# Second feed-forward of a two-layer kernel: the short last chunk's gate and value in one product, and every product over all 128 rows

## The chip, the cores and the metric

The kernel runs on one core of one Trainium2 chip. The metric is the device time of the whole program in microseconds (us), lower is better. TensorE (PE) multiplies, VectorE (DVE) and ScalarE (ACT) work element by element, GpSimd (POOL) and SyncE (SP) start transfers here; the five run side by side and are ordered by semaphores.

## The reference

Two layers, each an attention and a mixture of experts side by side, all in float32. The change is in the second layer's experts:

```python
H = _ffn_size(M)                                  # M = 128, H = 688
expert_inputs = jnp.einsum('GSEC,GSM->EGCM', dispatch, x)
layer_w0 = jnp.einsum('EGCM,EMH->EGCH', expert_inputs, w0_kernel)
layer_w1 = jnp.einsum('EGCM,EMH->EGCH', expert_inputs, w1_kernel)
hidden = jax.nn.gelu(layer_w0, approximate=True) * layer_w1
expert_outputs = jnp.einsum('EGCH,EHM->EGCM', hidden, wo_kernel)
```

There are 8 experts with 1024 slots each. w0 makes the gate, w1 the value, wo the output. Their inner width, 688, is five chunks of 128 and one of 48.

## The kernel before

The program is a row of stages, each a block in which every engine has its own instruction list; at a stage's end all engines meet. `ffn1_stage` is the second feed-forward. It takes the slots in two halves, and in each half the 8 experts one after the other: 16 steps of 512 slots, q = 0 to 15. Buffers are doubled by the step's parity i. The first pair of steps is written out, the rest is in a loop of pairs, and the last pair is written out again on PE and ScalarE.

A step on PE (`step`): for each of the six chunks u one product with w0 into `ps_a[u % 2]` (L1068) and one with w1 into `ps_b[u % 2]` (L1069), each 512 columns wide. In the trace these are `f1ps_a<-f1xT,f1w` and `f1ps_b<-f1xT,f1w`. Then come four transposes of the next step's input `xe` (L1058), and then the output product: for each of 4 tiles of 128 slots the six chunks of `hid` are multiplied with `wo` and accumulated in `ps_o` (L1079). A float32 product appears in the trace as two passes, so L1079 has 48 passes a step. `hrows(u)` is 128 for the first five chunks and 48 for the last: so the last L1068 and L1069 fill 48 columns of the array (written `128*48`), and every sixth L1079 uses 48 of its rows (`48*128`).

ScalarE takes the gelu of each `ps_a` into `ge` (L1107), then copies the transposed input into `xT` (L1099) and the output into `eo` (L1112). VectorE multiplies `ge` with `ps_b` into `hid` (L1135). PE starts L1079 when all six chunks of `hid` are there:

```python
pe.wait_ge(hid_ready, (q + 1) * HC)
```

SyncE loads w0, w1, wo in two pieces, and xe for the step after (L1016 to L1020, five DMAs on one semaphore, `NL = 5`), once the output product two steps back is done. PE waits for all five before the transposes. In the first pair of steps SyncE issues the copies for the next stage's attention behind the loads of experts 0 and 1. POOL stores `eo` (L1037).

Of the kernel before, what the change touches and what calls it, by code (L numbers as in the profile page):

```python
# [8 lines left out]
ALU = mybir.AluOpType  # L9
ACT = mybir.ActivationFunctionType  # L10
AX = mybir.AxisListType

P = 128
# [50 lines left out]
def up(n):  # L64

    return max(n, 0) if isinstance(n, int) else n


def rolled(eng, n, body):

    body(0)
    with eng.Fori(1, n) as i:
        body(i)
# [338 lines left out]
HID = int(8.0 * D) * 2 // 3  # L412
HID = HID + (8 - HID) % 8
HC = -(-HID // P)
# [541 lines left out]
def hrows(c):  # L956
    return min(P, HID - c * P)
# [19 lines left out]
def ffn1_stage(nc, w0_d, w1_d, wo_d, slots_dram, eo_dram, xn_all, send_ids, sent, ident, x_all, b_out, xnT_all, front, parts, one, bias_q, bias_k):  # L977
# [3 lines left out]
    GH = NG // 2  # L981
    N = GH * CAP
    PAIRS1 = 2 * E // 2
    with Pool(nc) as m:
        w0 = [m.sb(f"f1w0{i}", [P, HID]) for i in range(2)]
        w1 = [m.sb(f"f1w1{i}", [P, HID]) for i in range(2)]
        wo = [m.sb(f"f1wo{i}", [P, HC, D]) for i in range(2)]
        xe = [m.sb(f"f1xe{i}", [P, GH, D]) for i in range(2)]
        xT = [m.sb(f"f1xT{i}", [P, N]) for i in range(2)]
        ge = m.sb("f1ge", [P, 2, N])  # L990
        hid = m.sb("f1hid", [P, HC, N])
        eo = [m.sb(f"f1eo{i}", [P, GH, D]) for i in range(2)]
        ps_t = [m.ps(f"f1ps_t{i}") for i in range(2)]
        ps_a = [m.ps(f"f1ps_a{i}") for i in range(2)]
        ps_b = [m.ps(f"f1ps_b{i}") for i in range(2)]
        ps_o = [m.ps(f"f1ps_o{i}", (P, GH, D)) for i in range(2)]
        loaded = [m.sem(f"f1loaded{i}") for i in range(2)]
        xT_done, xT_ready = m.sem("f1xT_done"), m.sem("f1xT_ready")
        a_done, a_ready = m.sem("f1a_done"), m.sem("f1a_ready")
        b_done, hid_ready = m.sem("f1b_done"), m.sem("f1hid_ready")  # L1000
        o_done, o_ready = m.sem("f1o_done"), m.sem("f1o_ready")
        stored = [m.sem(f"f1stored{i}") for i in range(2)]
        biased = m.sem("f1biased")
        NL = 5
        xs_v = slots_dram.rearrange("(e g p) d -> e p g d", e=E, p=P)
        eo_v = eo_dram.rearrange("(e g p) d -> e p g d", e=E, p=P)
        full = (HC - 1) * P
        with nc.Block() as block:
            @block.sync
            def _(sp):  # L1010
                def experts(half, r):
                    for i in range(2):
                        e = r * 2 + i
                        g = slice(half * GH, (half + 1) * GH)
                        sp.wait_ge(o_done, up(half * E + e - 1))
                        sp.dma_start(w0[i][:, :], w0_d[bass.ds(e, 1)]).then_inc(loaded[i], 16)  # L1016
                        sp.dma_start(w1[i][:, :], w1_d[bass.ds(e, 1)]).then_inc(loaded[i], 16)
                        sp.dma_start(wo[i][:, 0:HC - 1, :], wo_d[bass.ds(e, 1), 0:full].rearrange("a (c p) d -> p (a c) d", p=P)).then_inc(loaded[i], 16)
                        sp.dma_start(wo[i][0:HID - full, HC - 1, :], wo_d[bass.ds(e, 1), full:HID]).then_inc(loaded[i], 16)
                        sp.dma_start(xe[i][:, :, :], xs_v[bass.ds(e, 1), :, g, :]).then_inc(loaded[i], 16)  # L1020
                    if half == 0 and isinstance(r, int):

                        send_parts(sp, front, parts, 0)
                        stack(sp, front, parts, 0, 0)

                sp.wait_ge(sent[0], 16 * NT)
                rolled(sp, E // 2, lambda r: experts(0, r))
                sp.wait_ge(sent[1], 16 * NT)
                rolled(sp, E // 2, lambda r: experts(1, r))

            @block.gpsimd
            def _(pool):
# [16 lines left out]
                for i in range(2):  # L1049
                    pool.wait_ge(stored[i], 16 * PAIRS1)  # L1050

            @block.tensor
            def _(pe):
                def transposes(R, i):
                    pe.wait_ge(loaded[i], (R + 1) * (16 * NL))
                    pe.wait_ge(xT_ready, up(R * 2 + i - 1))
                    for g in range(GH):
                        ins = nc.tensor.transpose(ps_t[i][:, g * P:(g + 1) * P], xe[i][:, g, :], ident[:, :])  # L1058
                    ins.then_inc(xT_done, 1)

                def step(R, i, last=False):
                    q = R * 2 + i
                    pe.wait_ge(xT_ready, q + 1)
                    for u in range(HC):
                        n = hrows(u)
                        pe.wait_ge(a_ready, up(q * HC + u - 1))
                        pe.wait_ge(hid_ready, up(q * HC + u - 1))
                        nc.tensor.matmul(ps_a[u % 2][0:n, :], w0[i][:, u * P:u * P + n], xT[i][:, :], start=True, stop=True).then_inc(a_done, 1)  # L1068
                        nc.tensor.matmul(ps_b[u % 2][0:n, :], w1[i][:, u * P:u * P + n], xT[i][:, :], start=True, stop=True).then_inc(b_done, 1)  # L1069
                    if not last:  # L1070
                        transposes(R + i, 1 - i)
                    pe.wait_ge(hid_ready, (q + 1) * HC)
                    pe.wait_ge(o_ready, up(q - 1))
                    if isinstance(R, int) and q == 1:
                        pe.wait_ge(front.sm["qk_ready"], 2)
                    for s in range(GH):
                        for c in range(HC):
                            n = hrows(c)
                            ins = nc.tensor.matmul(ps_o[i][:, s, :], hid[0:n, c, s * P:(s + 1) * P], wo[i][0:n, c, :],  # L1079
                                                   start=(c == 0), stop=(c == HC - 1))  # L1080
                    ins.then_inc(o_done, 1)

                def pair(R):
                    for i in range(2):
                        step(R, i)

                pe.wait_ge(front.sm["loaded"], 16 * 3)
                for n in range(2):
                    multiply_qk(nc, front, ps_o[n][:, :, :].rearrange("p (w j) d -> p w (j d)", w=2), xnT_all, n)
                transposes(0, 0)  # L1090
                rolled(pe, PAIRS1 - 1, pair)
                step(PAIRS1 - 1, 0)
                step(PAIRS1 - 1, 1, last=True)

            @block.scalar
            def _(a):
                def keep_T(R, i):
                    a.wait_ge(xT_done, R * 2 + i + 1)
                    nc.scalar.activation(xT[i][:, :], ps_t[i][:, :], ACT.Copy).then_inc(xT_ready, 1)  # L1099

                def step(R, i, last=False):
                    q = R * 2 + i
                    for u in range(HC):
                        n = hrows(u)
                        a.wait_ge(a_done, q * HC + u + 1)
                        a.wait_ge(hid_ready, up(q * HC + u - 1))
                        nc.scalar.activation(ge[0:n, u % 2, :], ps_a[u % 2][0:n, :], ACT.Gelu_apprx_tanh).then_inc(a_ready, 1)  # L1107
                    if not last:
                        keep_T(R + i, 1 - i)
                    a.wait_ge(o_done, q + 1)  # L1110
                    a.wait_ge(stored[i], R * 16)
                    nc.scalar.activation(eo[i][:, :, :], ps_o[i][:, :, :], ACT.Copy).then_inc(o_ready, 1)  # L1112

                def pair(R):
                    for i in range(2):
                        step(R, i)
                        if isinstance(R, int) and i == 0:
                            keep_qk(nc, a, front, ps_o[1][:, :, :].rearrange("p (w j) d -> p w (j d)", w=2), bias_q, bias_k, 1)

                keep_qk(nc, a, front, ps_o[0][:, :, :].rearrange("p (w j) d -> p w (j d)", w=2), bias_q, bias_k, 0)  # L1120
                keep_T(0, 0)
                rolled(a, PAIRS1 - 1, pair)
                step(PAIRS1 - 1, 0)
                step(PAIRS1 - 1, 1, last=True)

            @block.vector
            def _(v):
                def pair(R):
                    for i in range(2):
                        q = R * 2 + i  # L1130
                        for u in range(HC):
                            n = hrows(u)
                            v.wait_ge(a_ready, q * HC + u + 1)
                            v.wait_ge(b_done, q * HC + u + 1)
                            nc.vector.tensor_tensor(hid[0:n, u, :], ge[0:n, u % 2, :], ps_b[u % 2][0:n, :], ALU.mult).then_inc(hid_ready, 1)  # L1135

                rolled(v, PAIRS1, pair)


# [697 lines left out]
```

## Time and profile before

| what | value |
|---|---|
| median of 3 runs | 1888.92 us (1887.74 to 1889.97) |
| profiled execution, its own time | 1885.4 us |
| its span, first to last instruction | 1883.7 us |
| PE busy in the span | 1722.3 us (91%) |
| VectorE, ScalarE, POOL busy | 918.6, 764.0, 296.5 us |
| mean granted PE clock | 0.970 of full |
| second feed-forward in the span | from 928.6 to about 1242 us |

Times in the rows below are microseconds from the start of the span. Row by row, a group of instructions has its start, its duration from first start to last end, its engine, source line, output and inputs, and in brackets the idle time before it with what ended it. The granted clock is a share of 2.4 GHz: 1.00 or 0.50.

### The profile page before, as it was taken

Reading aid. Unit: us, or ns where it says so; the run is one execution under the profiler, and the core shown is the slowest. Engines: PE = TensorE matmul, PEld = TensorE weight load, DVE = VectorE, ACT = ScalarE, POOL = GpSimd, SP = SyncE. Lnnn points to the kernel's source line nnn. Section 1 sums busy time; section 2 is a strip of 40 time slices with the busy share of each in tenths; the row PEclk is TensorE's granted clock in tenths of the full one; section 3 lists DMA queues with packets and bytes.
Section 4 is the critical chain, followed back from the end, with each engine's and each line's share of the span. In section 5 each row is a group of like instructions: output and inputs, shape, how many; then the busy total and the mean of one; then the engine's idle time right before and its main releaser. Section 6 shows DMA issues by size and latency. Waiting matters only on the chain. (4 is left out here: it accounts for less than half of the span.)

```text
span 1883.7 us, 38993 instructions
## 1 busy us (share of the span) xinstructions
PE 1722.3 (91%) x13304; PEld 1307.1 (69%) x13304; DVE 918.6 (49%) x3193; ACT 764.0 (41%) x2111; POOL 296.5 (16%) x375
## 2 busy tenths in 40 slices
PE   3698999999999999999699999959999999999896
PEld 3466778888888888888455555537777777777775
DVE  4323554545454555555321222236767666676664
ACT  1333222222222222222222222247767677776773
POOL 1001020101010101010240000003222322232222
PEclk9899999999999999999799999979999999999998
DMA  1201920000000000000232232248777777777775
GB/s 45 60 0 13 104 60 7 12 1 12 0 11 0 11 0 11 0 11 1 74 105 83 86 94 74 73 143 230 223 220 223 200 219 214 222 220 194 225 223 159
DMA packets 228518, 181.82 MB, mean 97 GB/s; under 512 B 80287, under 2 KB 217337, under 8 KB 228336
## 3 DMA queue, kind: packets, MB, share of 16 engines
q1 hardware_dynamic: 222962, 167.14, 33.6%
q0 software_dynamic: 5376, 12.44, 2.2%
q8 instruction: 94, 1.54, 0.4%
q14 instruction: 86, 0.70, 0.1%
HBM read 103.60 MB, written 75.78 MB: 95 GB/s over the span
## 5 line engine op out<-in xcount | busy, mean ns | idle before, releaser
L757 DVE TENSOR_TENSOR a0MT<-a0ps_M,mask 128x384 f32<-128x384 f32 x256 | 142.5, 557 | 259.4 <-PE a0ps_M L606 259.3
L1561 DVE CUSTOM_DVE_ANT_0 a1Pm<-a1ps_S,a1Sb 128x256 f32<-128x256 f32 x512 | 195.9, 420 | 147.7 <-issue 143.8
L1499 ACT ACTIVATE a1Pm<-a1Pm,a1nmx 128x256 f32<-128x256 f32 x512 | 254.6, 503 | 1.3 <-DVE a1nmx L1561 1.3
L701 ACT ACTIVATE a0qk<-a0ps_qk 128x512 f32<-128x512 f32 x128 | 76.5, 597 | 423.5 <-PE a0ps_qk L582 423.5
L1494 ACT ACTIVATE a1Rt<-a1ps_R 128x384 f32<-128x384 f32 x264 | 128.9, 488 | 170.0 <-PE a1ps_R L1369 164.7
L1135 DVE TENSOR_TENSOR f1hid<-f1ge,f1ps_b 128x512 f32<-128x512 f32 x96 | 65.9, 687 | 234.4 <-PE f1ps_b L1069 234.4
L1388 PE MATMUL a1ps_T<-ident,a1Pm 128*128 128x128 f32 x1024 | 163.0, 283 | 0.0
L604 PE MATMUL a0ps_M<-a0AT 128*128 128x256 f32 x512 | 153.9, 382 | 0.0
L752 DVE TENSOR_TENSOR a0AT<-a0ps_A,mask 128x384 f32<-128x384 f32 x256 | 130.8, 552 | 37.7 <-PE a0ps_A L591 37.7
L582 PE MATMUL a0ps_qk<-xnT_all,a0w_in 128*128 (+1 forms) x512 | 144.7, 405 | 1.4 <-PEq L310 1.4
L1378 PE MATMUL a1ps_S<-a1stk 72*128 72x256 bf16 x512 | 104.0, 286 | 22.0 <-issue 22.0
L1388 PEld LDWEIGHTS a1ps_T<-ident,a1Pm 128*128 128x128 f32 x1024 | 119.1, 146 | 2.2 <-ACT a1Pm L1499 0.2
L1369 PE MATMUL a1ps_R<-rel_st,a1stk 72*128 72x192 bf16 x528 | 91.9, 258 | 28.7 <-ACT a1Rt L1494 18.1
L1079 PE MATMUL f1ps_o<-f1wo,f1hid 128*128 128x128 f32 (+1 forms) x768 | 111.6, 291 | 5.1 <-DVE f1hid L1135 5.1
L1079 PEld LDWEIGHTS f1ps_o<-f1wo,f1hid 128*128 128x128 f32 (+1 forms) x768 | 95.1, 190 | 23.1 <-DVE f1hid L1135 6.2
L605 PEld LDWEIGHTS a0ps_M<-a0AT 128*128 128x128 f32 x512 | 97.9, 191 | 13.4
L582 PEld LDWEIGHTS a0ps_qk<-xnT_all,a0w_in 128*128 128x128 f32 x512 | 86.7, 189 | 23.4 <-issue 1.5
L1068 PE MATMUL f1ps_a<-f1xT,f1w 128*128 128x512 f32 x192 | 101.7, 611 | 0.7 <-ACT f1xT L1099 0.7
L1499 ACT ACTIVATION_READ_ACCUMULATOR a1Pm<-a1Pm,a1nmx 128x1 f32 x512 | 99.4, 194 | 0.0
L606 PE MATMUL a0ps_M<-a0AT 128*128 128x128 f32 x512 | 99.1, 275 | 0.0
L1069 PE MATMUL f1ps_b<-f1xT,f1w 128*128 128x512 f32 x192 | 98.9, 597 | 0.0
L605 PE MATMUL a0ps_M<-a0AT 128*128 128x128 f32 x512 | 98.8, 275 | 0.0
(236 smaller groups left out, 3061.0 us busy)
## 6 DMA issues: line engine op xcount, KB each, us to landing
skew<-a1Rt SPq DMA_DIRECT2D x132, 384.0 KB, 3.6
a1Sb<-skew SPq DMA_DIRECT2D x131, 384.0 KB, 4.9
f1w<-in_L_ffn_w_kernel SPq DMA_DIRECT2D x32, 344.0 KB, 3.4
a1stk<-parts SPq DMA_DIRECT2D x51, 192.0 KB
a1stk<-parts SPq DMA_DIRECT2D x153, 64.0 KB
parts<-a1prt SPq DMA_DIRECT2D x18, 384.0 KB, 4.7
f1wo<-in_L_ffn_wo_kernel SPq DMA_DIRECT2D x16, 320.0 KB, 4.2
slots<-zeros SPq DMA_DIRECT2D x8, 512.0 KB, 14.9
```

The costliest lines, as they stand in the source:

```text
L582: ins = nc.tensor.matmul(ps_qk[:, i, :], w_in[:, i, p * P:(p + 1) * P], xnT_all[:, bass.ds(b * T, T)], start=True, stop=True)
L604: nc.tensor.matmul(ps_M[h][:, 0:T], AT[h][:, 0:P], AT[h][:, 0:T], start=True, stop=True)
L605: nc.tensor.matmul(ps_M[h][:, T:HB], AT[h][:, P:T], AT[h][:, P:T], start=True, stop=False)
L752: nc.vector.tensor_tensor(AT[h][:, :], ps_A[h][:, 0:HB], mask[:, :], ALU.mult).then_inc(A_ready, 1)
L757: nc.vector.tensor_tensor(MT[h][:, :], ps_M[h][:, 0:HB], mask[:, :], ALU.mult).then_inc(M_ready, 1)
L1068: nc.tensor.matmul(ps_a[u % 2][0:n, :], w0[i][:, u * P:u * P + n], xT[i][:, :], start=True, stop=True).then_inc(a_done, 1)
L1079: ins = nc.tensor.matmul(ps_o[i][:, s, :], hid[0:n, c, s * P:(s + 1) * P], wo[i][0:n, c, :], start=(c == 0), stop=(c == HC - 1))
L1378: ins = nc.tensor.matmul(ps_S[hp % 2][:, n, :], stk[par][:, 0, h, it * P:(it + 1) * P], stk[par][:, 1, h, :], start=True, stop=True)
L1388: ins = nc.tensor.transpose(ps_T[k % 2][:, n, jt, :], Pm[:, place(2 * k + n), jt * P:(jt + 1) * P], ident[:, :])
L1494: nc.scalar.activation(Rt[:, hp, :, :], ps_R[:, :, :].rearrange("p n c -> p c n"), ACT.Copy).then_inc(sm["R_ready"], 1)
L1499: nc.scalar.activation(Pm[:, place(h), :], Pm[:, place(h), :], ACT.Exp, bias=nmx[it][:, h:h + 1], scale=-1.0, accum_out=den[it][:, h:h + 1 ...
L1561: nc.vector.tensor_tensor_reduce(out=Pm[:, place(h), :], in0=ps_S[hp % 2][:, n, :], in1=bias_of(it, hp, n), scale=-1.0, scalar=3.0e38, op0 ...
```

## The change

The two weights w0 and w1 stand in one buffer `w[i]`: 688 gate columns, 16 zero columns, the last 48 value columns, then the first 640 value columns. So the 128 columns from 640 on are the last 48 of the gate, 16 zeros, the last 48 of the value, and 16 columns of the value's first chunk. The last chunk needs one product, into `ps_a`, which has gate results on partitions 0 to 47 and value results on 64 to 111. ScalarE reads its gelu from partitions 0 to 47 and writes `ge` on 64 to 111, and VectorE multiplies there and writes `hid` there. The last chunk of `wo` is loaded to the same partitions; the other rows of `wo` and `hid` in that chunk are cleared once by VectorE at the start of the stage, and L1079 multiplies 128 rows in every chunk. SyncE waits for the clearing, and has six DMAs a step instead of five.

```diff
-        w0 = [m.sb(f"f1w0{i}", [P, HID]) for i in range(2)]
-        w1 = [m.sb(f"f1w1{i}", [P, HID]) for i in range(2)]
+        w = [m.sb(f"f1w{i}", [P, 2 * HID + PAD]) for i in range(2)]
...
-        NL = 5
+        cleared = m.sem("f1cleared")
+        NL = 6
...
-                        sp.dma_start(w0[i][:, :], w0_d[bass.ds(e, 1)]).then_inc(loaded[i], 16)
-                        sp.dma_start(w1[i][:, :], w1_d[bass.ds(e, 1)]).then_inc(loaded[i], 16)
+                        sp.dma_start(w[i][:, 0:HID], w0_d[bass.ds(e, 1)]).then_inc(loaded[i], 16)
+                        sp.dma_start(w[i][:, VALUE:VALUE + full], w1_d[bass.ds(e, 1), :, 0:full]).then_inc(loaded[i], 16)
+                        sp.dma_start(w[i][:, HID + PAD:VALUE], w1_d[bass.ds(e, 1), :, full:HID]).then_inc(loaded[i], 16)
-                        sp.dma_start(wo[i][0:HID - full, HC - 1, :], wo_d[bass.ds(e, 1), full:HID]).then_inc(loaded[i], 16)
+                        sp.dma_start(wo[i][UP, HC - 1, :], wo_d[bass.ds(e, 1), full:HID]).then_inc(loaded[i], 16)
...
+                sp.wait_ge(cleared, 1)
                 sp.wait_ge(sent[0], 16 * NT)
...
-                        nc.tensor.matmul(ps_a[u % 2][0:n, :], w0[i][:, u * P:u * P + n], xT[i][:, :], start=True, stop=True).then_inc(a_done, 1)
-                        nc.tensor.matmul(ps_b[u % 2][0:n, :], w1[i][:, u * P:u * P + n], xT[i][:, :], start=True, stop=True).then_inc(b_done, 1)
+                        nc.tensor.matmul(ps_a[u % 2][:, :], w[i][:, u * P:(u + 1) * P], xT[i][:, :], start=True, stop=True).then_inc(a_done, 1)
+                        if u < HC - 1:
+                            nc.tensor.matmul(ps_b[u % 2][:, :], w[i][:, VALUE + u * P:VALUE + (u + 1) * P], xT[i][:, :],
+                                             start=True, stop=True).then_inc(b_done, 1)
...
-                            n = hrows(c)
-                            ins = nc.tensor.matmul(ps_o[i][:, s, :], hid[0:n, c, s * P:(s + 1) * P], wo[i][0:n, c, :],
+                            ins = nc.tensor.matmul(ps_o[i][:, s, :], hid[:, c, s * P:(s + 1) * P], wo[i][:, c, :],
...
-                        nc.scalar.activation(ge[0:n, u % 2, :], ps_a[u % 2][0:n, :], ACT.Gelu_apprx_tanh).then_inc(a_ready, 1)
+                        nc.scalar.activation(ge[to, u % 2, :], ps_a[u % 2][of, :], ACT.Gelu_apprx_tanh).then_inc(a_ready, 1)
...
-                            nc.vector.tensor_tensor(hid[0:n, u, :], ge[0:n, u % 2, :], ps_b[u % 2][0:n, :], ALU.mult).then_inc(hid_ready, 1)
-
+                            nc.vector.tensor_tensor(hid[rows, u, :], ge[rows, u % 2, :], values[rows, :], ALU.mult).then_inc(hid_ready, 1)
+
+                for i in range(2):
+                    nc.vector.memset(w[i][:, HID:HID + PAD], 0.0)
+                    nc.vector.memset(wo[i][:, HC - 1, :], 0.0)
+                nc.vector.memset(hid[:, HC - 1, :], 0.0).then_inc(cleared, 1)
+                v.wait_ge(cleared, 1)
```

On PE, at the end of a step in the written-out first pair, there stood before:

```order
L1068 MATMUL f1ps_a<-f1xT,f1w 128x512
L1069 MATMUL f1ps_b<-f1xT,f1w 128x512
L1068 MATMUL f1ps_a<-f1xT,f1w 48x512
L1069 MATMUL f1ps_b<-f1xT,f1w 48x512
L1058 MATMUL f1ps_t<-ident,f1xe 128x128 x4
L1079 MATMUL f1ps_o<-f1wo,f1hid 128x128 x24
```

and now the same place reads, with the changed kernel's line numbers:

```order
L1074 MATMUL f1ps_a<-f1xT,f1w 128x512
L1076 MATMUL f1ps_b<-f1xT,f1w 128x512
L1074 MATMUL f1ps_a<-f1xT,f1w 128x512
L1065 MATMUL f1ps_t<-ident,f1xe 128x128 x4
L1086 MATMUL f1ps_o<-f1wo,f1hid 128x128 x24
```

One product of the two of the last chunk is gone, and the other has 128 columns of weights. The 24 products of L1079 are as many as before (their rows of the array don't show in this listing).

On VectorE, at the start of the stage and through its first step, there stands now:

```order
L1133 UNCONDITIONAL_BRANCH
L1146 MEMSET f1w 128x16
L1147 MEMSET f1wo 128x128
L1146 MEMSET f1w 128x16
L1147 MEMSET f1wo 128x128
L1148 MEMSET f1hid 128x512
L1143 TENSOR_TENSOR f1hid<-f1ge,f1ps_b 128x512 x5
L1143 TENSOR_TENSOR f1hid<-f1ge,f1ps_a 48x512
```

The five memsets are new, and the sixth product of the step reads `ps_a` where it read `ps_b`.

On SyncE, at the start of the stage, the loads of one expert were these five:

```order
L1016 DMA f1w<-in_L_ffn_w_kernel 128x688
L1017 DMA f1w<-in_L_ffn_w_kernel 128x688
L1018 DMA f1wo<-in_L_ffn_wo_kernel 128x5x128
L1019 DMA f1wo<-in_L_ffn_wo_kernel 48x128
L1020 DMA f1xe<-slots 128x4x128
```

and are now these six:

```order
L1021 DMA f1w<-in_L_ffn_w_kernel 128x688
L1022 DMA f1w<-in_L_ffn_w_kernel 128x640
L1023 DMA f1w<-in_L_ffn_w_kernel 128x48
L1024 DMA f1wo<-in_L_ffn_wo_kernel 128x5x128
L1025 DMA f1wo<-in_L_ffn_wo_kernel 48x128
L1026 DMA f1xe<-slots 128x4x128
```

The load of w1 is in two pieces, and the input `xe` is sixth in the row instead of fifth.

## Rows read from the trace of the kernel before

**Rows 1.** The page: PE's busy time, and its granted clock in 40 slices

```profile
PE 1722.3 (91%) x13304; PEld 1307.1 (69%) x13304; DVE 918.6 (49%) x3193; ACT 764.0 (41%) x2111; POOL 296.5 (16%) x375
...
PEclk9899999999999999999799999979999999999998
```

**Rows 2.** Busy time by stretch: stretch, length, each engine's busy us, clock, DMA

```profile
932.00:935.40 3.40, 0.27 (x1) 0.00 (x0) 0.00 (x0) 0.00 (x0) 2.79 (x3) 1.00 1.05 348
935.40:942.20 6.80, 5.45 (x9) 2.56 (x10) 0.45 (x1) 2.48 (x3) 4.97 (x7) 0.50 0.59 197
...
958.40:1237.00 278.60, 272.41 (x1138) 156.91 (x1136) 61.81 (x90) 72.19 (x122) 17.42 (x22) 1.00 0.27 82
```

**Rows 3.** Waits from 925 to 1240 us: total, times, longest

```profile
PE f1ps_o L1079 <- DVE f1hid L1135: 5.1, 16, 0.8
```

**Rows 4.** Timeline of PE around a step's short chunk and L1079

```profile
1013.90 1.13 PE L1068 MATMUL f1ps_a<-f1xT,f1w 128*128 128x512 f32 x2
...
1021.72 1.02 PE L1069 MATMUL f1ps_b<-f1xT,f1w 128*128 128x512 f32 x2
1022.68 1.06 PE L1068 MATMUL f1ps_a<-f1xT,f1w 128*48 128x512 f32 x2
1023.57 1.02 PE L1069 MATMUL f1ps_b<-f1xT,f1w 128*48 128x512 f32 x2
1024.53 0.66 PE L1058 MATMUL f1ps_t<-ident,f1xe 128*128 128x128 f32 x4
1025.52 6.97 PE L1079 MATMUL f1ps_o<-f1wo,f1hid 128*128 128x128 f32 x48 [0.33 <-DVE f1hid L1135]
1032.42 1.12 PE L1068 MATMUL f1ps_a<-f1xT,f1w 128*128 128x512 f32 x2
1033.38 1.02 PE L1069 MATMUL f1ps_b<-f1xT,f1w 128*128 128x512 f32 x2
1034.24 1.02 PE L1068 MATMUL f1ps_a<-f1xT,f1w 128*128 128x512 f32 x2
```

**Rows 5.** Timeline of ScalarE and VectorE for the same short chunk

```profile
1023.77 0.59 ACT L1107 ACTIVATE f1ge<-f1ps_a 48x512 f32<-48x512 f32 x1 [1.25 <-PE f1ps_a L1068]
...
1024.70 0.68 DVE L1135 TENSOR_TENSOR f1hid<-f1ge,f1ps_b 48x512 f32<-48x512 f32 x1 [1.16 <-PE f1ps_b L1069]
```

**Rows 6.** PE elsewhere: full passes alone, full and short; then L1079's mean pass

```profile
555.06 3.73 PE L628 MATMUL a0ps_g<-a0w_out,a0oT 128*128 128x128 f32 x32
...
137.20 1.16 PE L401 MATMUL f0ps_y<-f0w,f0hw 128*128 128x128 f32 x8
138.29 0.48 PE L403 MATMUL f0ps_y<-f0b,f0wT 8*128 8x128 f32 x2
138.70 1.16 PE L401 MATMUL f0ps_y<-f0w,f0hw 128*128 128x128 f32 x8
...
L1079 PE MATMUL f1ps_o<-f1wo,f1hid 128*128 128x128 f32 x40 | 5.5, 285 | 0.3 <-DVE f1hid L1135 0.3
```

**Rows 7.** Timeline at the start of this stage and of the next

```profile
928.67 0.34 SPq L1016 DMA_DIRECT2D f1w<-in_L_ffn_w_kernel  x1
...
930.58 0.42 SPq L1020 DMA_DIRECT2D f1xe<-slots  x1
...
936.06 1.12 PE L1058 MATMUL f1ps_t<-ident,f1xe 128*128 128x128 f32 x4 [3.79 <-DMA f1xe<-slots]
...
1242.63 0.34 SPq L1224 DMA_DIRECT2D parts<-a1prt  x1
...
1243.07 1.76 DVE L1632 MEMSET a1vx<- 128x2048 f32 x1 [14.41 <-PEq L1008]
1245.00 0.91 DVE L1633 MEMSET a1Sb<- 128x1024 f32 x1 [0.16 <-issue]
```

**Rows 8.** A load of f1xe in mid-stage, and all 16 from issue to landing

```profile
1016.19 0.38 SPq L1020 DMA_DIRECT2D f1xe<-slots  x1
...
DMA to landing us min/median/max: 4.0/5.0/6.7
```

More of the change, by code:

```diff
@@ L983, in ffn1_stage @@
     PAIRS1 = 2 * E // 2
+    full = (HC - 1) * P
+    SHORT = HID - full
+    PAD = P // 2 - SHORT
+    UP = slice(P // 2, P // 2 + SHORT)
+    VALUE = HID + PAD + SHORT
     with Pool(nc) as m:
-        w0 = [m.sb(f"f1w0{i}", [P, HID]) for i in range(2)]
-        w1 = [m.sb(f"f1w1{i}", [P, HID]) for i in range(2)]
+        w = [m.sb(f"f1w{i}", [P, 2 * HID + PAD]) for i in range(2)]
         wo = [m.sb(f"f1wo{i}", [P, HC, D]) for i in range(2)]
@@ L1003, in ffn1_stage @@
         biased = m.sem("f1biased")
-        NL = 5
+        cleared = m.sem("f1cleared")
+        NL = 6
         xs_v = slots_dram.rearrange("(e g p) d -> e p g d", e=E, p=P)
         eo_v = eo_dram.rearrange("(e g p) d -> e p g d", e=E, p=P)
-        full = (HC - 1) * P
         with nc.Block() as block:
@@ L1064, in step @@
                     for u in range(HC):
-                        n = hrows(u)
                         pe.wait_ge(a_ready, up(q * HC + u - 1))
                         pe.wait_ge(hid_ready, up(q * HC + u - 1))
-                        nc.tensor.matmul(ps_a[u % 2][0:n, :], w0[i][:, u * P:u * P + n], xT[i][:, :], start=True, stop=True).then_inc(a_done, 1)
-                        nc.tensor.matmul(ps_b[u % 2][0:n, :], w1[i][:, u * P:u * P + n], xT[i][:, :], start=True, stop=True).then_inc(b_done, 1)
+                        nc.tensor.matmul(ps_a[u % 2][:, :], w[i][:, u * P:(u + 1) * P], xT[i][:, :], start=True, stop=True).then_inc(a_done, 1)
+                        if u < HC - 1:
+                            nc.tensor.matmul(ps_b[u % 2][:, :], w[i][:, VALUE + u * P:VALUE + (u + 1) * P], xT[i][:, :],
+                                             start=True, stop=True).then_inc(b_done, 1)
                     if not last:
@@ L1103, in step @@
                     for u in range(HC):
-                        n = hrows(u)
+                        to, of = (slice(0, P), slice(0, P)) if u < HC - 1 else (UP, slice(0, SHORT))
                         a.wait_ge(a_done, q * HC + u + 1)
                         a.wait_ge(hid_ready, up(q * HC + u - 1))
-                        nc.scalar.activation(ge[0:n, u % 2, :], ps_a[u % 2][0:n, :], ACT.Gelu_apprx_tanh).then_inc(a_ready, 1)
+                        nc.scalar.activation(ge[to, u % 2, :], ps_a[u % 2][of, :], ACT.Gelu_apprx_tanh).then_inc(a_ready, 1)
                     if not last:
@@ L1131, in pair @@
                         for u in range(HC):
-                            n = hrows(u)
+                            rows, values = (slice(0, P), ps_b[u % 2]) if u < HC - 1 else (UP, ps_a[u % 2])
                             v.wait_ge(a_ready, q * HC + u + 1)
-                            v.wait_ge(b_done, q * HC + u + 1)
-                            nc.vector.tensor_tensor(hid[0:n, u, :], ge[0:n, u % 2, :], ps_b[u % 2][0:n, :], ALU.mult).then_inc(hid_ready, 1)
+                            if u < HC - 1:
+                                v.wait_ge(b_done, q * (HC - 1) + u + 1)
+                            nc.vector.tensor_tensor(hid[rows, u, :], ge[rows, u % 2, :], values[rows, :], ALU.mult).then_inc(hid_ready, 1)
[4 more added lines that the diff above has]
+                v.wait_ge(cleared, 1)
                 rolled(v, PAIRS1, pair)
```

## The prediction

> **What bounds the kernel now.** I read the page first: TensorE (PE) is busy for 91% of the span and its granted clock is near full everywhere [rows 1]. The change touches only the second feed-forward. I cut the trace at its edges and at the edges of the granted clock [rows 2]: from 958.4 to 1237.0 us PE is busy 272.4 of 278.6 us, always at clock 1.00 (2.4 GHz), while VectorE is busy 61.8 and ScalarE 72.2 us. So PE sets the pace there. In the list of waits for the stage [rows 3] PE waits for f1hid only 5.1 us in all, 16 times (once a step). What PE issues, and how densely, is the time of the stage.
>
> The PE timeline of one step [rows 4] shows how it is spent. Each 128x512 product is two passes (f32), and one product starts 0.86 us after the other (1033.38 to 1034.24). The step is 12 such products, 4 transposes, 48 passes of L1079, and takes 18.52 us (1013.90 to 1032.42). Look at the starts around the short chunk: 1021.72 to 1022.68 is 0.96, to 1023.57 is 0.89, to 1024.53 is 0.96: each change of shape adds 0.03 to 0.10. Then 48 passes of L1079 run from 1025.52 to the next L1068 at 1032.42, 6.90 us, or 144 ns a pass. Dense passes of the same size are quicker: the 32 passes of L628, all 128 rows, two accumulation groups of 16, take 3.73 us from first start to last end [rows 6]; less one pass of 0.285 us (mean of L1079) that is 31 gaps in 3.45 us, 111 ns.
>
> **The change, part by part.**
>
> 1. *The short chunk's product into f1ps_o gets 128 rows.* The nearest case of a short product among full ones is L403 (8 rows) among L401 [rows 6]: 8 full and 2 short passes recur every 1.50 us (137.20 to 138.70), where ten passes at 111 ns would be 1.115. The short product costs 0.385 us more than a full one. It is the passage that costs, not the rows' number: the two short passes begin at 138.29, the next full one at 138.70, 0.41 us for two. For our step: 48 gaps, of which the first after an idle engine stays 0.21, is 47 x 0.1115 + 0.21 = 5.45 us against 6.90: 1.45 saved. The next L1068 also ends its wait behind a short shape: its two passes take 0.96 to the next product (1032.42 to 1033.38) against 0.86, 0.10 more saved. Together 1.55; the other way, 4 x 0.385 = 1.54. I take 1.55 a step.
>
> The Trainium skill has two rules here. "TensorEngine Tiling (Array Packing)", section Tiling Modes, says that a change of tiling mode drains the engine; "TensorE: Matmul & The Clock Gate", section on LDWEIGHTS, says that the number of rows does not matter to a weight load, which taken alone speaks against any gain from zero rows. By the second alone this term would be 0, by the first it is what the rows show; the trace agrees with the first, at about 0.1 us for each passage.
>
> 2. *One product instead of two for the short chunk.* On PE this removes one L1069 (0.89 us) and the 0.10 and 0.10 of the passages, 1.09 in all. Little of it can be kept: the L1079 group waits for the last f1hid. That chain is now f1ps_a, gelu, product on VectorE. From the rows of both engines [rows 5]: the gelu of the short chunk starts 1.09 after its f1ps_a product (1022.68 to 1023.77) and takes 0.59; the VectorE product takes 0.68 and PE goes on 0.14 after its end (1025.38 to 1025.52). With the product at 1022.58: gelu 1023.67 to 1024.26, VectorE (hand-over not shown here; between 0 and 0.14, I take 0.05) 1024.31 to 1024.99, L1079 at 1025.13 instead of 1025.52. Saved: 0.39; with the bounds of the hand-over 0.30 to 0.44. PE then stands idle about 1 us between the transposes and L1079, where it was 0.33. No row shows a gelu that reads partitions 0 to 47 and writes 64 to 111; nothing in the rows prices it but the 0.59 of the unshifted one. If it or the VectorE operation took its time twice, 0.6 a step would go; I take no extra cost.
>
> Per step 1.55 + 0.39 = 1.94, and 16 steps: 31.0 us.
>
> 3. *Clearing and the sixth load, at the stage's start.* SyncE now waits for five memsets before its first DMA, and PE's first transposes wait for that load [rows 7]: issued 928.67 to 930.58, used at 936.06, after 3.79 us of idle PE. At the start of the next stage VectorE begins 0.44 us after SyncE (1242.63, 1243.07). A memset of 2048 elements a partition takes 1.76 and one of 1024 0.91, so 0.83 ns an element and 0.06 for each: 16, 128, 16, 128 and 512 elements make 0.07 + 0.17 + 0.07 + 0.17 + 0.48 = 0.96; gaps of 0 to 0.16 between them (1244.83 to 1245.00) make it 0.96 to 1.6. With the 0.44 and 0.1 for the signal the loads start 1.5 to 2.1 later. The sixth DMA pushes f1xe back by one issue, (930.58 - 928.67)/4 = 0.48. So PE starts 2.0 to 2.6 later. But it starts at clock 0.50 [rows 2], until 942.2. If the clock still rises then, a delay of 2.3 loses only 1.15, since half speed is what is lost. If it rises one 3.4 us stretch later, the loss is 2.9. I take 2.0, bounds 1.1 to 2.9.
>
> 4. *Later loads.* SyncE issues six DMAs a step. f1xe was issued at 1016.19 and lands 5.0 us later in the median, 6.7 at most [rows 8]: 1021.2, at most 1022.9, for transposes at 1024.53. Now it lands 0.48 later for transposes 1.19 earlier, so 1021.7 (at most 1023.4) against 1023.34, and PE's idle microsecond hides another 0.9. This costs nothing. POOL's queue is not touched.
>
> Sum: 31.0 - 2.0 = 29.0 us. The profiled execution is 1885.4 us (span 1883.7 and 1.7 around it) and would become 1856.4; it lies 3.5 below the median of the runs, 1888.9. I put the saving against the median: 1859.9, and forecast **1860 us**.
>
> **The rivals.**
>
> - *Zero rows bring nothing*: the excess in L1079 belongs to the boundary of accumulation groups. Then only term 2 is left: 16 x 0.39 - 2.0 = 4.2, so 1884.7. For it: in L1079 the short product always stands at such a boundary, as in L403. Against: L628 has one in its 32 passes and still runs at 111 ns. 4%.
> - *The loads come late*: 128 pieces of 192 bytes more, six issues. If f1xe landed 8.5 us after its issue (1025.2), it would be 0.95 past the 1024.24 from which PE feels it: 15 us lost, 1875. Nothing in the landing times of before (6.7 at most) reaches there. 5%.
> - *The clock falls, and it gets slower*: each step now has an idle microsecond next to the transposes. In the rows the clock was at 0.50 after PE had been nearly idle from 932.0 to 935.4 (0.27 us busy). Each microsecond at half clock costs 0.5, so the saving of a step is gone when 3.9 us of it run so. One stretch of 6.8 us in each step, as in 935.4 to 942.2, would cost 3.4 - 1.94 = 1.5 a step: 1860 + 16 x 3.4 = 1914. Against: an idle of 1 us is far below 3.4, and the rest of the step is dense. 3%.
> - *The shifted gelu or the 48-row product from f1ps_a is slow*: 0.6 a step, 1870. 6%.
>
> **How the numbers follow.** The forecast has 82%. Its own range: term 1 is known to 0.05 a step, term 2 to 0.1, together 2.4 us; the start 1; the granted clock in the attention stage that follows changes places when all moves 29 us, and a stretch of 3.4 us at half clock costs up to 1.7, a few of them more or less 3 to 4 us. That is 1854 to 1866. To take in half of the slow chain and of the late loads I give 1854 to 1870. Differences over 0.2% (3.8 us) can be told from no change. The first two and the fourth rival are all still faster (1884.7 is 0.22% below), the first of them just: faster 0.94, same 0.03, slower 0.03.
>
> **What would show it.** In the profile after: the passes of L1079 (now one form) start to next product in 5.4 to 5.5 us; a step of 16.5 us; one idle of PE near 1.0 us a step, ended by f1hid, about 16 us in all where 5.1 were; f1ps_b in 160 instead of 192 passes; first transposes near 938.4; VectorE waiting on ScalarE's f1ge 16 times; clock 1.00 throughout the steps. I would be wrong if L1079 stayed near 6.9 us, if transposes waited for f1xe in each step, or if clock 0.50 appeared between 960 and the stage's end.

## The result and the profile after

The changed kernel takes 1856.15 us (median of 4 runs, 1853.29 to 1862.72) against 1889.45 for the kernel before (4 runs). The ratio is 0.9828, 95% interval 0.9813 to 0.9844: 33.3 us faster where 29 were forecast, and inside the range of 1854 to 1870. Measured once more it was 0.985 (0.983 to 0.987), 1859.18 against 1887.12: 27.9 us faster.

The profiled execution took 1857.91 us, its span 1856.3. The page after, beside [rows 1]:

```profile
span 1856.3 us, 38958 instructions
...
PE 1681.9 (91%) x13272; PEld 1301.4 (70%) x13272; DVE 921.0 (50%) x3198; ACT 763.5 (41%) x2111; POOL 296.7 (16%) x375
...
PEclk9899999999999999999889999979999999999998
```

PE is busy 40 us less and keeps its share. The timeline of PE over one step after, beside [rows 4]:

```profile
990.23 1.02 PE L1074 MATMUL f1ps_a<-f1xT,f1w 128*128 128x512 f32 x2
991.09 1.02 PE L1076 MATMUL f1ps_b<-f1xT,f1w 128*128 128x512 f32 x2
...
997.95 1.02 PE L1076 MATMUL f1ps_b<-f1xT,f1w 128*128 128x512 f32 x2
998.81 1.02 PE L1074 MATMUL f1ps_a<-f1xT,f1w 128*128 128x512 f32 x2
999.67 0.60 PE L1065 MATMUL f1ps_t<-ident,f1xe 128*128 128x128 f32 x4
1001.24 5.62 PE L1086 MATMUL f1ps_o<-f1wo,f1hid 128*128 128x128 f32 x48 [0.97 <-DVE f1hid L1143]
1006.70 1.02 PE L1074 MATMUL f1ps_a<-f1xT,f1w 128*128 128x512 f32 x2
```

The 48 passes of the output product now take 5.46 us to the next product (1001.24 to 1006.70) where they took 6.90; the next product's passes begin 0.86 apart, not 0.96; the passages around the last chunk are gone (997.95, 998.81, 999.67: 0.86 each). This step takes 16.47 us (990.23 to 1006.70). Steps take two lengths in turn, 16.47 and 16.55, and before it was 18.45 and 18.52; the means are 16.504 and 18.477. PE now idles 0.97 before the output product. ScalarE and VectorE in the same place, beside [rows 5]:

```profile
999.87 0.59 ACT L1114 ACTIVATE f1ge<-f1ps_a 48x512 f32<-48x512 f32 x1 [1.12 <-PE f1ps_a L1074]
...
1000.49 0.69 DVE L1143 TENSOR_TENSOR f1hid<-f1ge,f1ps_a 48x512 f32<-48x512 f32 x1 [0.79 <-ACT f1ge L1114]
```

The gelu that moves partitions 0 to 47 to 64 to 111 takes 0.59 like the one that did not, and hands over to VectorE within 0.03 us. The waits of the stage after, beside [rows 3]:

```profile
PE f1ps_o L1086 <- DVE f1hid L1143: 15.4, 15, 1.4
...
PE f1ps_t L1065 <- DMA f1xe<-slots: 5.6, 2, 4.6
```

The start of the stage, beside [rows 7]:

```profile
928.75 0.07 DVE L1146 MEMSET f1w<- 128x16 f32 x1 [0.34 <-PEq L513]
928.81 0.17 DVE L1147 MEMSET f1wo<- 128x128 f32 x1
928.92 0.07 DVE L1146 MEMSET f1w<- 128x16 f32 x1
928.97 0.17 DVE L1147 MEMSET f1wo<- 128x128 f32 x1
929.19 0.48 DVE L1148 MEMSET f1hid<- 128x512 f32 x1
...
929.71 0.34 SPq L1021 DMA_DIRECT2D f1w<-in_L_ffn_w_kernel  x1
...
932.09 0.42 SPq L1026 DMA_DIRECT2D f1xe<-slots  x1
...
936.99 1.12 PE L1065 MATMUL f1ps_t<-ident,f1xe 128*128 128x128 f32 x4 [4.57 <-DMA f1xe<-slots]
```

The clearing takes 0.92 us from first start to last end, the first load is issued 1.04 later than before, f1xe 1.51 later (932.09 to 930.58), but the transposes start only 0.93 later: they come 4.9 us after the load's issue instead of 5.5. That 0.93 holds for this pair of profiles. In a second pair the transposes came 8.15 us after the stage's first product, against 6.45 before, which is 1.70 later.

### The profile page after: what moved, and what is told of

It is laid out like the page before. It is cut to its first block and busy times, and to the rows that moved or that the text cites. A ratio compares the mean times of both kernels' runs of the same rounds, so it can differ in the third digit from the quotient of the medians.

```text
span 1856.3 us, 38958 instructions
## 1 busy us (share of the span) xinstructions
PE 1681.9 (91%) x13272; PEld 1301.4 (70%) x13272; DVE 921.0 (50%) x3198; ACT 763.5 (41%) x2111; POOL 296.7 (16%) x375
## 5 line engine op out<-in xcount | busy, mean ns | idle before, releaser
L1143 DVE TENSOR_TENSOR f1hid<-f1ge,f1ps_b 128x512 f32<-128x512 f32 x80 | 55.0, 688 | 191.0 <-PE f1ps_b L1076 182.4
L1086 PE MATMUL f1ps_o<-f1wo,f1hid 128*128 128x128 f32 x768 | 89.9, 277 | 15.4 <-DVE f1hid L1143 15.4
L1086 PEld LDWEIGHTS f1ps_o<-f1wo,f1hid 128*128 128x128 f32 x768 | 87.0, 192 | 19.6 <-DVE f1hid L1143 11.9
L1418 PE MATMUL a1ps_X<-a1PT,tabs 128*128 128x256 f32 x384 | 96.1, 387 | 0.0
```

Of the source, the lines that this page charges most:

```text
L1086: ins = nc.tensor.matmul(ps_o[i][:, s, :], hid[:, c, s * P:(s + 1) * P], wo[i][:, c, :], start=(c == 0), stop=(c == HC - 1))
L1418: ins = nc.tensor.matmul(ps_X[k % 2][:, n, :, :], tabs[:, t, :], PT[it][:, jt, :, ig * GI:(ig + 1) * GI], start=(q == 0), stop=(q == len(u ...
```

## Experiments

Times are medians of 4 runs (10 for one product alone, 12 for the repeat of the kernel before). Ratios are to the kernel before, measured beside each. "Step" is the mean distance between the first products of steps 3 to 15 in the trace.

**Zero rows alone.** In the kernel before only the output product is changed, with the clearing that it needs:

```diff
-                            n = hrows(c)
-                            ins = nc.tensor.matmul(ps_o[i][:, s, :], hid[0:n, c, s * P:(s + 1) * P], wo[i][0:n, c, :],
+                            ins = nc.tensor.matmul(ps_o[i][:, s, :], hid[:, c, s * P:(s + 1) * P], wo[i][:, c, :],
```

> The kernel before, with the zero rows alone: wo and hid cleared, L1079 over 128 rows in every chunk; gate and value of the short chunk stay two products. Theory (the passages between a short and a full product are what L1079 pays): its 48 passes take about 5.45 us from first start to the next product where they took 6.90, and a step takes 18.48 - 1.55 = 16.93 us. With 0.5 us lost at the start, about 24 us faster than the kernel before. Rival (the excess sits at the boundary of accumulation groups): a step stays at 18.5 us and the time at that of before.

Its PE timeline:

```profile
1000.67 0.66 PE L1060 MATMUL f1ps_t<-ident,f1xe 128*128 128x128 f32 x4
1001.58 5.62 PE L1080 MATMUL f1ps_o<-f1wo,f1hid 128*128 128x128 f32 x48 [0.26 <-DVE f1hid L1136]
1007.04 1.02 PE L1070 MATMUL f1ps_a<-f1xT,f1w 128*128 128x512 f32 x2
1007.90 1.02 PE L1071 MATMUL f1ps_b<-f1xT,f1w 128*128 128x512 f32 x2
...
1014.77 1.02 PE L1071 MATMUL f1ps_b<-f1xT,f1w 128*128 128x512 f32 x2
1015.72 1.06 PE L1070 MATMUL f1ps_a<-f1xT,f1w 128*48 128x512 f32 x2
1016.62 1.02 PE L1071 MATMUL f1ps_b<-f1xT,f1w 128*48 128x512 f32 x2
1017.57 0.66 PE L1060 MATMUL f1ps_t<-ident,f1xe 128*128 128x128 f32 x4
1018.56 5.62 PE L1080 MATMUL f1ps_o<-f1wo,f1hid 128*128 128x128 f32 x48 [0.34 <-DVE f1hid L1136]
```

Step 16.931 us against 18.477: 1.546 less, to the hundredth the 1.55 forecast. The four group boundaries (where one accumulation ends and the next begins) are all still there and cost nothing; the rival falls. The passages of the 48-column products remain (0.95, 0.90, 0.95). Time: 1867.36 us, ratio 0.9893 (0.9867 to 0.9918), 19.2 us under the 1886.59 beside it, where 24 were expected; the stage itself is 24.2 shorter than in the first profile of before and 22.0 than in the second.

**One product alone.** The changed kernel with the short rows put back into the output product:

```diff
-                            ins = nc.tensor.matmul(ps_o[i][:, s, :], hid[:, c, s * P:(s + 1) * P], wo[i][:, c, :],
+                            k = slice(0, P) if c < HC - 1 else UP
+                            ins = nc.tensor.matmul(ps_o[i][:, s, :], hid[k, c, s * P:(s + 1) * P], wo[i][k, c, :],
```

> The changed kernel, but the output product's last chunk uses only the 48 rows 64 to 111 (same results). Theory: only the chain's gain stays, 0.42 us a step as in the trace after (its output product starts 2.43 us after the last f1ps_a product; before, 2.84 us after a product that itself stood 0.1 later): steps of about 18.0 us, in all 6 us faster than before. Rival (removing one product of 0.86 us and two passages frees PE by 1.1 us a step): 17.4 us a step, 17 us faster.

```profile
1002.59 0.60 PE L1065 MATMUL f1ps_t<-ident,f1xe 128*128 128x128 f32 x4
1004.16 6.98 PE L1087 MATMUL f1ps_o<-f1wo,f1hid 128*128 128x128 f32 x48 [0.97 <-DVE f1hid L1144]
1011.07 1.13 PE L1074 MATMUL f1ps_a<-f1xT,f1w 128*128 128x512 f32 x2
```

Step 18.052 us, 0.425 less than before: the chain's gain and no more. Of the 1.1 us that PE no longer works, 0.97 stands as idle ahead of the output product, where 0.33 were. The output product is back at 6.91. Time: 1883.29, ratio 0.9977 (0.9961 to 0.9994), 3.3 us faster where 6 were expected; the stage is 6.7 shorter than in the first profile of before, 4.5 than in the second. The two parts add up: 1.546 + 0.425 = 1.971, and the full change gives 18.477 - 16.504 = 1.973.

**112 rows instead of 128.** As the last, with `slice(0, UP.stop)` for the short chunk.

> The changed kernel, but the output product's last chunk uses rows 0 to 111 (of 128) instead of all. If what costs is the change between a product of at most 64 rows and one of more, 112 rows cost nothing: steps of 16.51 us as in the changed kernel. If every change in the number of rows costs, steps of about 18.0 us, 25 us slower than the changed kernel.

A step's output product and the next product, then the groups of the stage by shape:

```profile
1005.27 5.62 PE L1087 MATMUL f1ps_o<-f1wo,f1hid 128*128 128x128 f32 x48 [0.97 <-DVE f1hid L1144]
1010.73 1.02 PE L1074 MATMUL f1ps_a<-f1xT,f1w 128*128 128x512 f32 x2
...
L1087 PE MATMUL f1ps_o<-f1wo,f1hid 128*128 128x128 f32 x640 | 83.5, 277 | 15.4 <-DVE f1hid L1144 15.4
...
L1087 PE MATMUL f1ps_o<-f1wo,f1hid 112*128 112x128 f32 x128 | 24.7, 274 | 0.0
```

Step 16.504 us, the changed kernel's to the nanosecond; 1859.38 us, ratio 0.9849 (0.9822 to 0.9875). A product of 112 rows among products of 128 is free, one of 48 or 8 is not. Where between 48 and 112 rows the cost begins, no run here shows.

**The wait for the sixth chunk, later.** The changed kernel, where PE waits for five chunks of hid before the output product and for the sixth ahead of its first use:

```diff
-                    pe.wait_ge(hid_ready, (q + 1) * HC)
+                    pe.wait_ge(hid_ready, q * HC + HC - 1)
...
+                            if s == 0 and c == HC - 1:
+                                pe.wait_ge(hid_ready, q * HC + HC)
```

> The changed kernel, but PE starts the output product when five chunks of hid are there and waits for the sixth only ahead of the first product that reads it. Theory (after the change the chain gelu, product on VectorE is the only thing PE waits for in a step, 1.0 us): it starts right behind the transposes, about 1.1 us a step is saved, steps of 15.4 us, 17 us faster than the changed kernel. Rival (the chain sets the pace and the wait only moves on to the sixth product): half of the gain, 8 us.

```profile
1009.37 1.02 PE L1074 MATMUL f1ps_a<-f1xT,f1w 128*128 128x512 f32 x2
...
1010.23 0.60 PE L1065 MATMUL f1ps_t<-ident,f1xe 128*128 128x128 f32 x4
...
1010.66 2.51 PE L1088 MATMUL f1ps_o<-f1wo,f1hid 128*128 128x128 f32 x20
...
1011.05 0.69 DVE L1145 TENSOR_TENSOR f1hid<-f1ge,f1ps_a 48x512 f32<-48x512 f32 x1 [0.79 <-ACT f1ge L1116]
```

The output product starts 0.43 us after the transposes do, with no idle, while VectorE is still to make the sixth chunk. VectorE ends it at 1011.74, and the eleventh pass, the first that reads it, would start about 1011.8 (1010.66 and ten passes of 0.11): it comes just in time. Step 15.357 us, 1.147 less. 1840.39 us, ratio 0.9751 (0.9725 to 0.9777), and 0.9768 (0.9725 to 0.9811) when measured again. One thing shows that the cover is gone: in the second step the transposes wait for their load,

```profile
964.22 0.66 PE L1065 MATMUL f1ps_t<-ident,f1xe 128*128 128x128 f32 x4 [1.98 <-DMA f1xe<-slots]
```

and that step takes 17.44 us instead of 15.36. In the second profile of this kernel the wait was 2.35 us, the granted clock then stood at 0.50 for 3.4 us (from 967.95), and the step took 19.44. So the fall of the clock that the prediction had as a rival for every step did come, once, in another kernel; behind the wait of 1.98 us in the first profile it did not, and not behind one of 2.92 us in the kernel with all three. The changed kernel waits in the same step,

```profile
967.83 0.66 PE L1065 MATMUL f1ps_t<-ident,f1xe 128*128 128x128 f32 x4 [1.03 <-DMA f1xe<-slots]
```

and its step of 16.49 us is no longer than the others (16.47 and 16.55 in turn), since PE would have idled there. In its second profile the wait was 1.35 and the step 16.82, so there 0.35 us stuck out.

**The clearing off the load's path.** The changed kernel, but in the first step SyncE waits for the clearing only ahead of the short piece of wo.

> The changed kernel, but SyncE waits for the clearing only ahead of the one load that touches cleared rows (the short piece of wo). Theory (the clearing costs what it delays the first load): first load at 928.7 instead of 929.7, first transposes 0.5 to 1 us earlier, which at half clock is worth 0.3 to 0.9 us of the total; not to be told from the changed kernel in the timing, only in the trace. Rival (the first load of xe is bound by the transfers already queued): first transposes unchanged near 937.0.

The first transposes came 6.58 us after the stage's first product, against 8.27 in the changed kernel; but the first step took 18.94 instead of 18.39, and the whole stage 283.2 against 283.3. The timing, 1857.02 us with ratio 0.9839 (0.9803 to 0.9875), can't be told from the changed kernel's. Since the first transposes of the kernel before stand at 7.42 in one profile and 6.45 in another, these profiles do not settle how much of the 1.69 us is the clearing. They do show where the lead went: the second step took 17.54 us instead of 16.49, because its transposes waited 2.07 us for their load. SyncE issues that load behind the copies for the attention, and these begin 21.6 to 21.7 us after the stage's first product in every profile, whether PE is early or late. The awaited transposes come 39.01 us after the stage's first product here and 39.11 in the changed kernel. So time won at the stage's start is mostly waited away in its second step.

**Zero rows in the first feed-forward.** The changed kernel, where the bias product of 8 rows becomes one of 128, both operands cleared once:

```diff
-        b2s = m.sb("f0b2", [E, D])
+        b2s = m.sb("f0b2", [P, D])
...
-        wT = m.sb("f0wT", [E, GT])
+        wT = m.sb("f0wT", [P, GT])
...
+                nc.vector.memset(wT[:, :], 0.0)
+                nc.vector.memset(b2s[:, :], 0.0).then_inc(f0cleared, 1)
```

> The changed kernel, with the same zero rows for another stage: in the first feed-forward the bias product of 8 rows (L403) becomes one of 128 rows, with its two operands cleared once. Theory (0.385 us for each such product among full ones, 32 of them): 8 full and 2 former short passes recur every 1.115 us instead of 1.50, 12 us in all if PE bounds that stage; 10 to 12 us faster than the changed kernel. Rival (the stage waits for VectorE and ScalarE, the gain turns into idle of PE): the passes are quicker but the stage as long as before.

Its PE timeline, beside [rows 6]:

```profile
128.49 1.06 PE L405 MATMUL f0ps_y<-f0w,f0hw 128*128 128x128 f32 x8
129.38 0.39 PE L407 MATMUL f0ps_y<-f0b,f0wT 128*128 128x128 f32 x2
129.60 1.06 PE L405 MATMUL f0ps_y<-f0w,f0hw 128*128 128x128 f32 x8
```

Ten passes recur every 1.11 us (128.49 to 129.60) instead of 1.50. 1845.71 us, ratio 0.9786 (0.9753 to 0.9819): 10.4 less than the changed kernel's 1856.15, 13.5 less than its 1859.18, and 11.3 less than the 1857.02 of the last experiment, which was measured beside it. The traces are cleaner than the medians: from the first f0ps_y pass to the last pass of that stage it is 95.2 us in the first profiles of before and after, and 83.7 in the kernel with all three, 11.5 less, with the clock at 1.00 in each. The 10 to 12 expected hold; PE bounds that stage.

**All three together.**

> The changed kernel with the late wait for the sixth chunk, the clearing off the load's path, and the zero rows in the first feed-forward together. If the three are independent: 17 + 0.5 + 11 = 28 us faster than the changed kernel, 1828 us. If the first feed-forward gives nothing: 1839 us.

1827.56 us (1825.82 to 1828.50), ratio 0.9685 (0.9652 to 0.9718): 62.1 us under the kernel before (1889.65), and 28.6 under the changed kernel's 1856.15 (31.6 under its 1859.18), where the sum was 28. It is the fastest version found.

**What is chance.** The kernels before and after were profiled and timed again:

> The kernel before, unchanged, profiled once more. Theory (the part of a difference that lies in the attention stage at the end is chance, since the granted clock falls at other places from one execution to the next): the second feed-forward again takes 314.1 us within 0.3, the attention stage differs from the 640.9 of the first profile by some us. Rival (the attention stage is as repeatable as the rest, so its 3.4 us more in the changed kernel belong to the change): 640.9 within 0.5.

> The changed kernel, unchanged, profiled once more, against the kernel before in five rounds. Theory: the second feed-forward again takes 283.3 us within 0.5, the attention stage differs from 644.3 by some us; the ratio lies at 1 - 30.9/1887 = 0.9836 within its interval. Rival (the change costs or gives something in the attention stage): a stage of 644.3 again and a ratio off 0.9836 by more than its interval.

and two of the others:

> The kernel with the zero rows alone, unchanged, profiled and timed once more. Its first profile had 648.8 us in the attention stage, where the kernel before has 640.9 and 641.0, and its median was 19 us below the kernel before where its second feed-forward was 24 us shorter. If the attention stage is chance, it lies elsewhere this time; if it belongs to the kernel (the same code begins at another moment of the transfers), it is 648.8 within 1 again.

> The kernel with the late wait, unchanged, profiled and timed once more. Its first profile had 646.4 us in the attention stage. Chance: elsewhere between 640 and 650 this time. The kernel's own: 646.4 within 1. The second feed-forward is 266.7 us within 0.5 either way.

From all traces: the second feed-forward (first product of the stage to the first of the next), the attention stage behind it to the end, whose code is the same in all, and how long the clock was at 0.50 in that attention stage, in us:

```
kernel                  2nd feed-forward   attention   at half clock
before                       314.1           640.9         67.5
before, again                311.9           641.0         67.6
after                        283.3           644.3         70.9
after, again                 283.8           641.8         71.7
zero rows alone              289.9           648.8         82.2
zero rows alone, again       290.0           644.6         74.6
one product alone            307.4           642.7         69.3
112 rows                     283.5           647.3         77.3
late wait                    266.7           646.4         76.3
late wait, again             268.8           642.4         69.0
clearing aside               283.2           645.1         71.7
first feed-forward too       284.4           640.8         70.8
all three                    267.7           641.1         64.3
```

The attention stage moves by up to 8 us between kernels, and by 0.1 to 4.2 between two profiles of one. It is longest where the clock was longest at half: the zero rows alone had 14.7 us more of half clock than before, which by an estimate (half speed loses half the time where PE is busy) is worth up to 7.3 of their 7.9 us. The code ahead of the second feed-forward is no steadier: the eleven profiles that share it reach the stage 925.6 to 932.7 us after their start. The first feed-forward took 125.6 us in the repeats of before and after and 122.4 in their first profiles: in the repeats the clock was at 0.50 for its last 10 us.

So there is room for the few us between the gain in the stage and the gain in the median: 24.2 and 19.2 for the zero rows (20.1 when repeated), 30.9 and 33.3 for the change (28.1 and 27.9 when repeated). That they lie in these other stages is likely and not shown, since of each kernel's runs only one or two were profiled. The repeat of the kernel before came out at 1.0003 (0.9989 to 1.0018), so over a dozen runs its median repeats. For the zero rows alone both profiles lie above the 641 of before; whether that kernel draws longer stretches or had bad luck twice is open.

The expectations for the repeats were missed in three places. The second feed-forward of the kernel before took 311.9 where 314.1 within 0.3 was expected, and that of the late wait 268.8 where 266.7 within 0.5 was; the first has its cause at the stage's start, the second mainly in the clock's fall told above. And the attention stage of before, which was to differ by some us, repeated within 0.1: for this kernel the rival came true, for the other three that were profiled twice it fell.

## Why the prediction was right

**Step 1 (the zero rows)** was right in mechanism and size: 1.55 a step forecast, 1.546 measured alone. The row that carried it was the 8-row product of another stage, because it put the price on the passage and not on the number of rows. The starts of single passes in the trace of before say where the 0.385 us lie. Full passes start 0.112 us apart; around a short product the four distances are 0.205 (to its first pass), 0.213, 0.202 (back to a full one) and 0.213. So each of the two passages costs 0.19 us, spread over two distances of 0.1 each; the prediction's "about 0.1 us for each passage" is the excess of one distance, and its sum had the whole. The first distance behind an idle PE is 0.208 too: behind a change of shape the passes start as they do from rest.

The Trainium skill's rule that a change of tiling mode drains the engine ("TensorEngine Tiling (Array Packing)", Tiling Modes) agrees with this and with the run of 112 rows: that page lists row tilings of 64 and of 32 rows, which 112 rows do not fit, and they were free. That the chip takes a 48-row product for one of a tiled mode is concluded from this, not seen. The Trainium skill's other rule, that rows do not matter to a weight load ("TensorE: Matmul & The Clock Gate", LDWEIGHTS), is about true of the load alone (its mean is 191 ns for 128 and for 112 rows, 184 for 48) and says nothing of the passage.

**Step 2 (one product)** was right: 0.39 forecast, 0.425 measured. The hand-over to VectorE was 0.03 us and VectorE's to PE 0.06 (1001.18 to 1001.24) instead of the 0.14 of before. The rival of a slow shifted gelu fell, 0.59 as before. That PE idles 0.97 was forecast; that this idle was the next thing to take away was shown by the late wait, which gave 1.147 a step, nearly three times what the removed product gave.

**Step 3 (the start)** was mis-sized in its parts, and that its sum came out is luck. Expected were 1.5 to 2.1 us for the clearing; it was 1.04. VectorE started within 0.1 us of where SyncE had, not 0.44 later, and small memsets overlap instead of leaving gaps. The first transposes were expected near 938.4 and came at 936.99. From the stage's first product to the first product of the second step it was 29.84 and 27.62 us in the two profiles of before, and 28.47 and 28.64 in the two of after; with the 1.97 of the step's own gain, the start cost 0.6 by the first pair and 3.0 by the second. The 2.0 of the forecast lies between, the 3.0 just outside its bounds of 1.1 to 2.9. Most of the spread is that of the kernel before: in its first profile the clock had fallen for 6.8 us at the stage's start, in the repeat for 3.4 (in both profiles of after for 6.8), and in the repeat its first input landed 0.9 us sooner after its issue. Whether the change has a part in that, two pairs cannot say.

**Step 4 (the loads)** held for the steady steps and missed one place: the second step's load is issued behind the twelve copies for the attention, later after its predecessor than the others. PE waited 1.03 and 1.35 us for it in the two profiles of after, and the kernel before had waited there in its repeat, 0.36 us with five loads. In the first profile of after it cost nothing, for the reason given for the other steps, that PE would idle anyway; in the second it cost 0.35. The rival was real and nearly covered; the late wait took the cover away and it cost 2.1 us once and, with a fall of the clock, 4.1 the other time.

**The clock rival** fell for the changed kernel: the clock stood at 1.00 from 958.4 on through all steps, as it did in its second profile,

```profile
958.40:1206.20 247.80, 231.02 (x1104) 148.15 (x1102) 61.95 (x90) 71.15 (x120) 17.49 (x21) 1.00 0.30 93
```

with PE idle about 1 us in each of them.

In sum, the 31.0 for 16 steps was 31.6 (16 x 1.973). Less 0.6 at the start and 0.1 elsewhere, the stage is 30.9 shorter by the first pair of profiles. By the second it is 28.1: less 3.0 at the start, 0.35 in the second step and 0.1 elsewhere. The forecast of 29.0 lies between the two. The medians differ by 33.3, and by 27.9 when repeated, so the size of the first is more than the change gave in either pair of profiles. What the prediction had right is the steps; that the total came within 5 us owes something to the start and to where the clock fell.

## What to carry to other kernels

Where products of few rows (48 and 8 here) stand between full ones, and PE bounds the stage, count them: each short product cost 0.385 us more than a full one here, the time of three and a half dense 128x128 passes. Products of few columns cost less: each passage to or from 48 columns took 0.03 to 0.10 us. Filling the rows with zeros costs one clearing and no time on PE, and it worked again in another stage for 11.5 us. When a removal on the bounding engine leaves an idle ahead of one wait, look whether the work behind it needs all that the wait asks for: splitting it gave more than the product removed, until the next thing late (a load) showed. And before time is taken off a stage's start, look for what is issued at a fixed time behind it: here the copies held the second step's load back, and the lead was lost there.

## What the runs showed that I had not expected

- 112 rows among 128 are exactly free (step 16.504 us both), while 48 rows (from partition 0 or from 64) and 8 rows cost 0.385 to 0.387 us for each product between full ones.
- Five small memsets on VectorE took 0.92 us together, less than the sum of their durations in the profile (0.96).
- The same attention stage took 640.8 to 648.8 us, with 64.3 to 82.2 us of it at half clock.
- The copies for the attention begin 21.6 to 21.7 us after the stage's first product in every kernel, so the second step's load does not come earlier when PE does.
